# Attention scores from two fp16 parts, two heads in the two halves of TensorE's rows

## The reference

```
xn     = layernorm(x)
q,k,v  = split(xn @ w_qkv.T + b_qkv)
scores = q @ k.T / 4 + slope[h] * (key - 1023)      # ALiBi, per head
scores = -1e9 where key > query
s      = softmax(scores) @ v @ w_out.T + b_out
h      = silu(linear(xn, w_gate)) * linear(xn, w_up) # octonion, ternary weights, 1360 wide
out    = x + s * silu(linear(h, w_down))
```

## Time and profile before

| | |
|---|---|
| median of 3 runs | 966.93 us (963.75 to 967.62) |
| the profiled execution | 966.12 us, its span 964.3 us |
| busy in the span | PE 905.3, DVE 648.4, ACT 462.2, POOL 110.8 us |
| mean granted TensorE clock | 0.98 of full speed |
| moved by DMA | 92.41 MB |

### The profile page before, as it was taken

How to read it: one execution, slowest core, us unless ns; L and a number is a source line. 1 busy time by engine, 2 the same in 40 slices (tenths; PEclk the granted TensorE clock), 3 DMA queues, 4 the chain that set the end, 5 groups by cost and what they waited for, 6 DMA issues and landing times.

```text
span 964.3 us, 16724 instructions
## 1 busy us (share of the span) xinstructions
PE 905.3 (94%) x5630; PEld 483.2 (50%) x5630; DVE 648.4 (67%) x1425; ACT 462.2 (48%) x634; POOL 110.8 (11%) x119
## 2 busy tenths in 40 slices
PE   3696999999999996999999999999999999999987
PEld 3582457645854682444444444444444444443565
DVE  5678543543454442774888888888888888883488
ACT  3474532243223311124666666666666666667610
POOL 1121212130313032120000000000000000000042
PEclk9798999999999998999999999999999999999999
DMA  7322004201410138911256664546664456742757
GB/s 199 148 83 77 1 25 154 85 1 38 164 60 0 58 139 119 126 17 44 41 75 102 100 84 73 78 72 100 95 86 74 77 74 100 99 134 102 246 180 306
DMA packets 78177, 92.41 MB, mean 96 GB/s; under 512 B 26829, under 2 KB 43213, under 8 KB 78129
## 3 DMA queue, kind: packets, MB, share of 16 engines
q1 hardware_dynamic: 78017, 91.54, 43.7%
q0 software_dynamic: 112, 0.27, 0.2%
HBM read 57.57 MB, written 33.82 MB: 95 GB/s over the span
## 4 chain that ended last, share of the span: by engine, by line
PE 51%; DMA 3%; DVE 3%; issue 2%; ACT 1%; SPq 1%; DVEq 0%; ACTq 0%
PE psum L1285 15%; PE psum L1256 14%; PE psum L1269 12%; PE psum L1274 3%; DMA o_scr<-osum 2%; PE psum L250 2%; PE psum L251 2%; PE psum L1259 1%; PE psum L262 1%; PE psum L261 1%; DMA r_scr<-den 1%; DMA Ks<-r_scr 1%; ACT hid L278 1%; SPq L1022 0%; DVE mx L1150 0%
## 5 line engine op out<-in xcount | busy, mean ns | idle before, releaser
L1100 ACT ACTIVATE probs<-psum 128x1024 f32<-128x1024 f32 (+1 forms) x256 | 222.1, 915 | 108.3 <-PE psum L1274 91.1
L1150 DVE TENSOR_REDUCE mx<-psum 128x1 f32<-128x512 f32 (+2 forms) x352 | 224.8, 685 | 37.9 <-PE psum L1256 26.2
L1256 PE MATMUL psum<-Ks,Qs 99*128 99x512 bf16 (+3 forms) x768 | 203.8, 329 | 7.9 <-issue 5.6
L1269 PE MATMUL psum<-Qs,Ks 102*128 102x512 bf16 (+3 forms) x768 | 190.4, 326 | 2.1 <-DVE g_stage L306 1.6
L1146 DVE CUSTOM_DVE_ANT_0 mshown<-psum,ahead 128x384 bf16<-128x384 f32 (+1 forms) x256 | 149.2, 621 | 33.1 <-PE psum L1256 32.0
L250 PE MATMUL psum<-X,MG 128*128 128x512 f16 (+1 forms) x352 | 136.3, 387 | 5.0 <-PEq L324 3.7
L251 PE MATMUL psum<-X,MG 128*128 128x512 f16 (+1 forms) x352 | 136.1, 387 | 0.0
L1256 PEld LDWEIGHTS psum<-Ks,Qs 99*128 99x128 bf16 x768 | 62.5, 97 | 134.9 <-DVE mx L1146 51.5
L1285 PE MATMUL psum<-probs,Vs 128*32 128x512 f32 (+3 forms) x1152 | 126.2, 521 | 0.0
L1269 PEld LDWEIGHTS psum<-Qs,Ks 102*128 102x128 bf16 x768 | 73.8, 98 | 57.0 <-ACT probs L1100 8.4
L278 ACT ACTIVATE hid<-psum,sig_scale 128x512 f32<-128x512 f32 (+1 forms) x44 | 30.2, 687 | 146.7 <-PE psum L251 146.6
(11 more groups left out here) (128 smaller groups left out, 1128.5 us busy)
## 6 DMA issues: line engine op xcount, KB each, us to landing
Qs<-q_scr SPq DMA_DIRECT2D x96, 128.0 KB
Ks<-k_scr SPq DMA_DIRECT2D x96, 128.0 KB
o_scr<-osum SPq DMA_DIRECT2D x32, 256.0 KB, 4.1
q_scr<-qk_stage SPq DMA_DIRECT2D x16, 384.0 KB, 2.4
k_scr<-qk_stage SPq DMA_DIRECT2D x16, 384.0 KB, 2.5
v_scr<-v_stage SPq DMA_DIRECT2D x16, 256.0 KB, 2.0
g_scr<-g_stage SPq DMA_DIRECT2D x16, 256.0 KB, 2.0
Vs<-v_scr SPq DMA_DIRECT2D x16, 256.0 KB
```

The lines of the kernel that those rows point to most:

```text
L1100: nc.scalar.activation(probs[n % PSLOTS][:, 2 * pair:2 * pair + 2, 0:COLS[n]], s_bank[pair][:, :, 0:COLS[n]], ACT.Exp, scale=1.0 / INV_SCA ...
L1150: nc.vector.tensor_reduce(dst, m_bank[bank][:, 0:n * keys].rearrange("p (n k) -> p n k", n=n), AX.X, ALU.max).then_inc(max_read, 1)
L1256: last = nc.tensor.matmul(tile[:, hh, :], Qs[s][0:ROWS_MAX, h + hh, qb * P:(qb + 1) * P], Ks[s][0:ROWS_MAX, h + hh, k0:k0 + keys], start=( ...
L1269: last = nc.tensor.matmul(bank[:, at:at + cols], Ks[s][0:ROWS_ALL, 2 * pair + h, kb * P:(kb + 1) * P], Qs[s][0:ROWS_ALL, 2 * pair + h, (c ...
```

## The change

Queries and keys are multiplied by a power of two worked out from the weights and biases (`qk_scale`) and kept as two fp16 parts. Three pairs of parts are summed (high by high, high by low, low by high), so that a score product has 53 rows: 48, three of ALiBi, two of minus the maximum. That fits in 64 rows: head 2p lies in rows 0 to 63 and head 2p+1 in rows 64 to 127 of the same slot, and `scores` alternates between the two halves (u = 0, 1), which write different banks. A maximum tile comes from one half; tiles hold at most two heads, and there are 41 per quad. The masks are products of 64 rows, twice as many instructions. The exponential takes its scale from an SBUF column instead of a constant. In `interleave` a product comes ahead of its step's scores, and the wait for the maxima rows moves from the beginning of a quad to its first scores. ScalarE makes `rest`, VectorE casts it to part 0, GpSimd subtracts. In the preparation, ScalarE squares two weight blocks of 2048 columns, and VectorE works out the scales in 12 small instructions.

```diff
-TERM_Q = [0, 0, 1, 1, 0, 2]
-TERM_K = [0, 1, 0, 1, 2, 0]
-ROWS_QK = HD * len(TERM_Q)
+ROWS_QK = 3 * HD
 ROWS_MAX = ROWS_QK + 3
-ROWS_ALL = ROWS_MAX + 3
+ROWS_ALL = ROWS_MAX + 2
+HALF = P // 2
...
-            n = CH // keys
-            for h in range(0, QH, n):
-                out.append((qb, h, min(n, QH - h), CH * half, keys))
+            n = min(CH // keys, PAIRS)
+            for pair in range(0, PAIRS, n):
+                out += [(qb, u, pair, n, CH * half, keys) for u in range(2)]
+            if half and keys == P:
+                out[-1:] = [(qb, 1, pair, 1, CH * half, keys) for pair in range(PAIRS)]
...
     for n in range(NST):
-        main += [("scores", 0, (n, pair), 2 * COLS[n] + 2 * P * len(STEPS[n][1]) * (n in DIAG)) for pair in range(2)]
         if n >= LAG:
             main.append(("products", 0, n - LAG, 4 * COLS[n - LAG]))
         elif not first:
             main.append(("products", -1, NST + n - LAG, 4 * COLS[NST + n - LAG]))
+        main += [("scores", 0, (n, pair), COLS[n] + P * len(STEPS[n][1]) * (n in DIAG)) for pair in range(2)]
...
-                        act.wait_ge(qk_stored[m % 2], c * (KT * 16) + m // 2 * 16 + 16)
-                        nc.scalar.activation(qk_stage[m % 2][:, 0, :], bank_of(QK0 + m), ACT.Identity,
-                                             bias=bq_col[:, m:m + 1]).then_inc(q1_done, 1)
+                        act.wait_ge(q3_done, c * 2 * KT + m + 1)
+                        nc.scalar.activation(rest[m % 2][:], bank_of(QK0 + m), ACT.Identity, bias=bs_col[:, m:m + 1],
+                                             scale=qk_scale[:, m // KT:m // KT + 1]).then_inc(q1_done, 1)
...
+                for i in range(2):
+                    nc.scalar.activation(squares[i], wslot[i].rearrange("p t d -> p (t d)"), ACT.Square, accum_out=asum[:, 3 + i:4 + i]).then_inc(asum_done, 1)
+                    nc.scalar.activation(bsquares[:, KT * i:KT * (i + 1)], bq_col[:, KT * i:KT * (i + 1)], ACT.Square,
+                                         accum_out=asum[:, 5 + i:6 + i]).then_inc(asum_done, 1)
...
-                        nc.vector.scalar_tensor_tensor(out=rest[m % 2][:], in0=bank_of(QK0 + m), scalar=bq_col[:, m:m + 1],
-                                                       in1=qk_stage[m % 2][:, 0, :], op0=ALU.add, op1=ALU.subtract).then_inc(evac_done, 1)
-                        dve.wait_ge(evac_done, evacuated(c, QK0 + m))
-                        nc.vector.tensor_copy(qk_stage[m % 2][:, 1, :], rest[m % 2][:]).then_inc(q2_done, 1)
+                        dve.wait_ge(qk_stored[m % 2], c * (KT * 16) + m // 2 * 16 + 16)
+                        nc.vector.tensor_copy(qk_stage[m % 2][:, 0, :], rest[m % 2][:]).then_inc(evac_done, 1)
...
+                    for dst, scr, split in ((Qs, q_scr, 0), (Ks, k_scr, HD)):
+                        heads = scr[bass.ds(b, 1), :, bass.ds(hq * (QH * HD), QH * HD)].rearrange("a r (p u d) t -> u r d (a p) t", u=2, d=HD)
+                        for u in range(2):
+                            twice = dst[s][u * HALF + split:u * HALF + split + 2 * HD]
+                            once = 2 * HD - 2 * split
+                            for r in range(2):
+                                sp.dma_start(twice[r * HD:(r + 1) * HD], heads[u, r]).then_inc(stacked[s], 16)
+                            sp.dma_start(dst[s][u * HALF + once:u * HALF + once + HD], heads[u, 0]).then_inc(stacked[s], 16)
...
-                sp.dma_start(Qs[s][ROWS_MAX:ROWS_ALL], mrows[:]).then_inc(m_stacked, 16)
+                for u in range(2):
+                    sp.dma_start(Qs[s][u * HALF + ROWS_MAX:u * HALF + ROWS_ALL], mrows[u * QH * KB:(u + 1) * QH * KB]).then_inc(m_stacked, 16)
...
                 def scores(t, n, pair, s):
                     c, blocks = STEPS[n]
+                    if n == 0 and pair == 0:
+                        pe.wait_ge(m_stacked, t * 32 + 64)
                     pe.wait_ge(exp_done, t * (2 * NST) + 2 * n + pair + 1)
...
+                    for kb, at, cols in blocks:
+                        for u in range(2):
+                            rows = slice(u * HALF, u * HALF + ROWS_ALL)
+                            last = nc.tensor.matmul(s_bank[pair][:, u, at:at + cols], Ks[s][rows, pair, kb * P:(kb + 1) * P],
+                                                    Qs[s][rows, pair, (c + 1) * CH - cols:(c + 1) * CH], start=(at == 0), stop=n not in DIAG)
+                    if n in DIAG:
+                        apart = max(blocks[-1][1] // P, 1)
+                        for r in range(2):
+                            for u in range(2):
...
+                                last = nc.tensor.matmul(squares, causal[half, r], unit[half, 0, 0:HALF].unsqueeze(1).to_broadcast([HALF, len(blocks), HALF]),
+                                                        start=False, stop=(r == 1))
```

More of the change, by code:

```diff
@@ L339, in program @@
             gneg = TTs[0:GRP, 1].rearrange("p j o -> p (j o)")[:, 0:NG // 2]
-            qk_stage = [alloc(one, f"qk_stage{i}", [P, 3, CH], bf16) for i in range(2)]
+            qk_stage = [alloc(one, f"qk_stage{i}", [P, 2, CH], f16) for i in range(2)]
             rest = [alloc(one, f"rest{i}", [P, CH], f32) for i in range(2)]
@@ L351, in program @@
             bv_row = alloc(one, "bv_row", [P, D], f32)
-            asum = alloc(one, "asum", [P, 3], f32)
+            asum = alloc(one, "asum", [P, 7], f32)
             mean = alloc(one, "mean", [P, 3], f32)
+            bound = alloc(one, "bound", [P, 2], f32)
+            root = alloc(one, "root", [P, 2], f32)
+            qk_scale = alloc(one, "qk_scale", [P, 2], f32)
+            both = alloc(one, "both", [P, 1], f32)
+            inverse = alloc(one, "inverse", [P, 1], f32)
+            bs_col = alloc(one, "bs_col", [P, 2 * KT], f32)
+            c_rows = alloc(one, "c_rows", [P, (ROWS_MAX - ROWS_QK) * PAIRS * S // P], f16)
+            squares = [MD[:, KT * i:KT * (i + 1), :].rearrange("p k d -> p (k d)").bitcast(bf16) for i in range(2)]
+            bsquares = MD[:, 2 * KT, 0:2 * KT].bitcast(bf16)
             half = alloc(one, "half", [P, 3], f32)
@@ L793, in _ @@
                     if n == 3 * KT:
-                        pe.wait_ge(asum_done, 4)
+                        pe.wait_ge(asum_done, 8)
                         pe.wait_ge(xl_done, 2 * KT)
-                        nc.tensor.matmul(banks[0][:, 0:3], ones[:], asum[:], start=True, stop=True).then_inc(mean_ready, 1)
+                        nc.tensor.matmul(banks[0][:, 0:5], ones[:], asum[:, 0:5], start=True, stop=False)
+                        nc.tensor.matmul(banks[0][:, 3:5], ones[:], asum[:, 5:7], start=False, stop=True).then_inc(mean_ready, 1)
                 pe.wait_ge(wl_done, NWT)
@@ L865, in program @@
             den = alloc(two, "den", [P, NCH, P], f32)
-            Qs = [alloc(two, f"Qs{i}", [P, QH, S], bf16) for i in range(SLOTS)]
-            Ks = [alloc(two, f"Ks{i}", [P, QH, S], bf16) for i in range(SLOTS)]
+            QKs = [alloc(two, f"QKs{i}", [P, 2, PAIRS, S], f16) for i in range(SLOTS)]
+            Qs, Ks = ([x[:, i] for x in QKs] for i in range(2))
+            spare = [alloc(two, f"spare{i}", [P, KT, CH], f32) for i in range(3)]
             Vs = [alloc(two, f"Vs{i}", [P, KB, 2 * QH * HD], f32) for i in range(SLOTS)]
@@ L987, in _ @@
                 for i in range(SLOTS):
-                    sp.dma_start(Qs[i][ROWS_QK:ROWS_MAX], alibi[0:QH, ROWS_MAX - ROWS_QK:].rearrange("h r t -> r h t")).then_inc(q_ones, 16)
+                    for u in range(2):
+                        sp.dma_start(Qs[i][u * HALF + ROWS_QK:u * HALF + ROWS_MAX], c_scr).then_inc(q_ones, 16)
                 for i in range(SLOTS):
@@ L1100, in step @@
                             nc.scalar.activation(probs[n % PSLOTS][:, 2 * pair:2 * pair + 2, 0:COLS[n]], s_bank[pair][:, :, 0:COLS[n]],
[L1101 to L1102 removed]
+                                                 ACT.Exp, scale=exp_scale[:, 0:1]).then_inc(exp_done, 1)
+                        if n == LAG - 2 and not first:
                             copy_out(t - 1, 1, ENDS[1])
[L1104 removed]
+                        if n == ENDS[0] + LAG - 1:
                             copy_out(t, 0, ENDS[0])
@@ L1347, in alibi_parts @@
     for _ in range(3):
-        bits = rest.view(np.uint32) & np.uint32(0xFFFF0000)
-        parts.append((bits >> 16).astype(np.uint16))
-        rest = rest - bits.view(np.float32)
-    parts += [np.full((H, S), 0x3F80, np.uint16)] * 3
+        parts.append(rest.astype(np.float16))
+        rest = rest - parts[-1].astype(np.float32)
+    parts += [np.full((H, S), M_SCALE, np.float16)] * 2
     return np.ascontiguousarray(np.stack(parts, axis=1))
```

165 lines of the change are left out of this document (100 added, 65 removed).

## The result

The changed kernel takes 957.8 us (median of 16 runs, 946.09 to 962.8) against 966.8 for the kernel before on the same chip: ratio 0.989, interval 0.9865 to 0.9913. It is faster, as forecast, but by 9 us and not by 56, and the median lies outside the range of 896 to 938. The profiled execution is the fastest of its runs: 946.09 us, span 944.3.

The account below looks back on a forecast made before the run. TensorE bounds the kernel before, VectorE after at 25.4 us per quad. Terms -46.3 (quads 1 to 13), -2.8, -3.5, +1.5, -6 and +1 sum to -56.1 from 966.1: 910.0, median 0.8 above, so 911 us; range 896 to 938.

Parts of the forecast that it names:

- The two halves overlap: TensorE's score matmuls per quad: pairs in the two row halves run side by side, 3.9 us instead of 7.8.
- The sums of work: Busy time per quad after the change: TensorE 20.8 to 25.4 us, VectorE 24.2, ScalarE 20.8.
- ScalarE's 1.8 us more per quad: 20 exponentials per quad with a column as scale cost 0 to 1.8 us more, taken as 1.8, beside VectorE's work.
- The wait at the first maximum tile: Start of block two: TensorE's 5.58 us wait for slot 0 at 380.00 goes, -6 us (-3 to -8).
- The weight loads stay hidden: TensorE's score and mask pairs: a 97 ns weight load costs nothing; otherwise 4.7 us more per quad, chance 0.02.
- the signs that the prediction names: Trace signs: score pairs start almost together, quads repeat every 25.4 us, VectorE over 94% busy, no wait near 380, among others.
- I take 1.2 us of such waits: VectorE per usual quad: waits for TensorE's tiles add 1.2 us to 24.2 us of work, period 25.4 us.
- TensorE still sets the pace: Usual quads: maxima mostly alone, upper mask price, ring and exponential waits add up; period 27.0, 933 us in all; chance 0.20.
- about a quarter of its idle time now: Basis given for VectorE's 1.2 us of waits per quad; its slack before the change was 4.67 us.
- my upper bound of 27.0: Usual quad's period at most 27.0 us: TensorE's 25.4 plus a third of VectorE's 4.67 us of slack.
- The maxima rows come late: Between quads: copy and two DMAs take 5.0 us against about 4.7; 0.3 us wait gives 915, 2 us 939; chance 0.07.
- Small terms: Outside quads 1 to 13: up to quad 0 -5 us, quad 0 -2.8, quad 14 -3.5, quad 15 +1.5, closing part 0.

## Why the prediction was wrong in size

**Right.** The two halves overlap, and without that the changed kernel is slower than the kernel before (ratio 1.0494). The sums of work hold: VectorE is busy 23.63 us per quad (24.2 worked out), ScalarE 20.53 (20.8), TensorE 24.59, between 20.8 with all maxima in pairs and 25.4 with none. TensorE's figure is an upper bound of its work: a matmul's record lasts 0.38 us where the next may start after 0.22, so each gap in the stream counts as busy in part. ScalarE's 1.8 us more per quad measured 1.6 (20.53 against the 18.95 of the earlier trace rows), and they weren't fully hidden: 0.36 come through. The wait at the first maximum tile is gone (the chain of after, against the earlier trace rows; between these two lines it has one matmul behind another):

```profile
378.34 0.22 PE psum L268
381.57 0.23 PE psum L1325 x4
```

As forecast, TensorE's loads wait for VectorE's reads. The weight loads stay hidden. The Trainium skill (TensorE: Matmul & The Clock Gate, Part 3: Packing small matmuls) says that a load overlaps running matmuls only where its row group differs. By it, an estimate with the 0.09 us that a load takes in the profile, the two pairs of scores and two of masks at 858.22 would take some 0.7 us. They took 0.35: the row decides against it.

Of the signs that the prediction names, one held in part (6 of 24 score pairs start together in a usual quad) and two failed: the period, and VectorE busy for over 94% of it (87%).

**The failed step: "I take 1.2 us of such waits".** The period was put at 25.4 as VectorE's 24.2 plus 1.2 of waits; it is 27.05, VectorE's 23.63 plus 3.4. For 13 quads that is 13 x 1.65 = 21.5 us. I had taken VectorE as the pace with a margin. The runs show that neither engine is one. Relieving VectorE alone gives 2.0 us, TensorE alone 0.95, ScalarE alone 0.36, and placing the same work otherwise moves the period between 25.6 and 27.1. The number of the rival "TensorE still sets the pace" came true (27.0), its mechanism in part: the maxima do run mostly alone, and the waits on ring and exponentials do add up, but TensorE is idle for 2.4 us of the period and taking its masks away gives 0.95 us. With three busy sums of 24.6, 23.6 and 20.5 us and rings of three tiles and one bank pair between them, my reading is that each engine's list must fit the others' phase, and that what doesn't fit adds up. My "about a quarter of its idle time now" was a guess from a kernel in which one engine had no idle time, and no row of that profile shows the 1.2. The period came out at my upper bound of 27.0; that the bound was met so closely is luck, as its terms (25.4 for TensorE and a third of VectorE's slack) aren't what the period is made of.

**The step that was missing: the loop.** Nothing in the prediction speaks of `pe.Fori`. A back jump with a stop costs 6.0 us. The profiled execution has one. The median would have three, and then 18 us of the 47 between 911 and 957.8 are theirs; the loop written out gave back 15 to 17. In each stop TensorE stands for 4.6 us, VectorE and ScalarE run dry behind it, and the clock is at 1.2 GHz afterwards. I priced the kinds of wait that the trace of before showed, and this one it didn't show. The runs show what it is: at a jump with a stop TensorE's instructions are fetched again, nine packets of 16 KB for the turn, and at a jump without one none are. It is gone without the loop, there at one, two or three of the three jumps with it, and gone with the loop, and the fetches with it, when VectorE's reads or the masks are cut down. It is smaller when the scores lie ahead of the product (4.2 to 5.1). What decides at a jump whether the instructions have to be fetched again, no run shows: one kernel, the changed one, has jumps of both kinds.

**The rival "the maxima rows come late".** Forecast at 0.3 to 2 us; in the new order it doesn't appear in the lists, with the scores first it is 0.9 to 1.0 us each quad, and `LEAD` 13 removes it together with the whole 0.98 us of the period (26.65 to 25.67).

**Small terms.** Quad 0 is 4.0 us worse than forecast, the time up to it 2.4, quad 14 1.3, the closing part 2.3, quad 15 1.3 better. Together with 21.5 and 6.0 that is the 36.1 us between the forecast's -56.1 and the -20.0 of the profiled span; two more stops would bring the profiled execution to the median. None of the small terms was tested.

**What stays open.** What makes a jump fetch its turn again. And which hand-over sets 27.0 us in the new order: the places of `parts` (27.12) and of the lead (27.00) don't move it, its order of scores and product does only together with `LEAD` (26.65, 25.67). That the phase decides is argued from six orders of the same work, not shown by a run that changes one ring.

## What to carry to other kernels

When a change takes work from the engine that sets the pace, the next bound is not the busy sum of the second engine: where three engines come within a few microseconds of each other and trade small buffers in fixed lists, allow the gap of the whole old slack, and expect the order to need a new search (`LEAD` 13 was worth 16 us with the scores first, and nothing in the new order or before the change). A hardware loop that costs nothing can begin to cost with a change elsewhere: look at the instruction queues in the DMA view, and compare with the loop written out, before you judge the change. When two executions of one kernel differ, compare their traces period by period, and their packet counts.

## What the runs showed of the hardware

- At a back jump of TensorE's loop it stood for 3.7 to 4.8 us with "issue", in some turns of some executions and not in others; a jump with a stop cost 4.2 to 6.6 us in all, 9 to 12 with both heads in one half. The kernel before has the same loop and no such stop.
- Each such stop went with nine packets of 16 KB on the instruction queue q8 (28, 37, 46 and 55 for no, one, two and three stops); at jumps without a stop there were none, and none from 552 to 820 us in the kernel before.
- Code without a loop, fetched the whole time (45 packets), had no stop.
- After a stop TensorE's granted clock was 0.50: for 3 us with the pairs side by side, and for over 11 us when both heads shared a half, though it was busy for all of these 11.
- Score matmuls in the two halves of the rows, with nothing between, took about half the time: four of 384 columns and two pairs of masks in 0.35 us, with their weight loads hidden. Between maximum matmuls only 6 of 24 pairs started together.
- TensorE's busy time for the same matmuls was 24.3 to 25.5 us per quad, by their order.
